# A graph layer on one core: adding stores, list ends on two queues, edges loaded as 112 and 13 rows, keys joined in five passes

## The reference, cut to what matters

```python
xn = _layernorm(x)                                   # x: 6250 nodes x 256
x = x + gnn(xn, edge_index) + mix(xn[None])[0]       # 200000 edges, sorted by dst in the input
x = x + ffn(_layernorm(x)[None])[0]
# gnn: w = sigmoid(relu(xn[col] @ W1 + b1) @ W2 + b2);  sums of w * xn[col] and of w by row, one over the other
# mix: linear attention over 8 heads of 32 columns, one 32x32 product a head over all nodes
# ffn: softmax router, the best two of 6 experts a node, their outputs weighted and summed:
h1 = relu(features @ expert_w1 + expert_b1)          # 256 -> 256, each expert
h2 = relu(h1 @ expert_w2 + expert_b2)
expert_out = h2 @ expert_w3 + expert_b3
combined = sum(expert_out[top_i] * routing_weights)
```

## Time and profile before

| | us |
|---|---|
| median of 3 runs | 1731.37 (1729.7 to 1732.82) |
| the profiled execution | 1728.47 |
| its span, first to last instruction | 1726.7 |
| busy: PE | 1428.3 (83%) |
| busy: DVE | 1354.0 (78%) |
| busy: ACT | 811.1 (47%) |
| busy: POOL | 665.5 (39%) |
| mean granted TensorE clock | 0.925 of full |

### The profile page before, as it was taken

How to read it: one execution, slowest core, us unless ns; L and a number is a source line. 1 busy time by engine, 2 the same in 40 slices (tenths; PEclk the granted TensorE clock), 3 DMA queues, 4 the chain that set the end, 5 groups by cost and what they waited for, 6 DMA issues and landing times.

```text
span 1726.7 us, 40180 instructions
## 1 busy us (share of the span) xinstructions
PE 1428.3 (83%) x12059; PEld 1329.7 (77%) x12059; DVE 1354.0 (78%) x3945; ACT 811.1 (47%) x1983; POOL 665.5 (39%) x669
## 2 busy tenths in 40 slices
PE   0147878646559999999999999999999399999896
PEld 0136777535559999999999999999999399998786
DVE  8998879889958788878888888888887556666565
ACT  1114556336625455555555555555555155555453
POOL 1563565664411222222222222222222323338777
PEclk9767889767779999999999999999999699999998
DMA  7000000003334111111011101110111344433442
GB/s 187 11 1 1 1 1 1 1 18 122 119 105 122 45 41 39 43 41 44 34 49 37 49 34 49 37 48 34 46 40 46 129 135 144 130 102 108 123 129 73
DMA packets 68547, 108.68 MB, mean 63 GB/s; under 512 B 14306, under 2 KB 47849, under 8 KB 68231
## 3 DMA queue, kind: packets, MB, share of 16 engines
q1 hardware_dynamic: 50726, 57.78, 11.9%
q0 software_dynamic: 17760, 50.16, 8.3%
HBM read 52.41 MB, written 57.47 MB: 64 GB/s over the span
## 4 chain that ended last, share of the span: by engine, by line
PE 60%; issue 15%; DVE 11%; POOL 7%; DMA 3%; ACT 1%; SPq 1%; DVEq 1%; another core or an unknown queue 0%; POOLq 0%; ACTq 0%
PE turned L1400 17%; PE front L1400 17%; PE turned L1382 9%; DVE sort_mem L1704 7%; POOL acc_mem L781 6%; PE turned L1541 4%; PE front L1541 4%; PE front L1561 3%; PE front L1429 1%; PE front L1422 1%; PE turned L1534 1%; DMA gath_mem<-in_dst 1%; DVE sort_mem L1801 1%; DVE sort_mem L1712 1%; ACT a_ring L1138 1%
## 5 line engine op out<-in xcount | busy, mean ns | idle before, releaser
L1801 DVE TENSOR_TENSOR sort_mem<-lane_bf,sort_mem 128x512 bf16<-128x512 bf16 x1372 | 519.0, 420 | 145.6 <-PE turned L1382 131.6
L1138 ACT ACTIVATE a_ring<-turned 128x384 fp32r<-128x384 f32 (+1 forms) x686 | 373.4, 544 | 408.9 <-PE turned L1382 405.3
L1400 PE MATMUL turned<-y_all,a_ring 128*128 128x258 f32 x2450 | 387.1, 296 | 8.8 <-ACT a_ring L1138 8.8
L1400 PE MATMUL front<-y_all,a_ring 128*128 128x258 f32 x2352 | 377.4, 297 | 1.1 <-ACT a_ring L1138 1.1
L1704 DVE TENSOR_TENSOR sort_mem<-sort_mem 128x320 f32<-128x320 f32 (+2 forms) x568 | 325.6, 634 | 3.0
L1400 PEld LDWEIGHTS turned<-y_all,a_ring 128*128 128x128 f32 x2450 | 317.5, 190 | 12.9 <-issue 11.2
L1400 PEld LDWEIGHTS front<-y_all,a_ring 128*128 128x128 f32 x2352 | 306.1, 190 | 4.7 <-ACT a_ring L1138 1.4
L1382 PE MATMUL turned<-sort_mem 128*128 128x128 bf16 (+1 forms) x2695 | 259.6, 217 | 3.8 <-DVE sort_mem L1801 2.0
L1382 PEld LDWEIGHTS turned<-sort_mem 128*128 128x128 bf16 x2695 | 139.6, 98 | 40.3 <-DVE sort_mem L1801 9.2
L1339 PE MATMUL turned<-ident,sort_mem 128*128 128x128 f32 x286 | 57.8, 368 | 105.9 <-DVE sort_mem L1704 105.2
L855 POOL TENSOR_TENSOR feat_mem<-feat_mem,ln_eps 128x1 f32<-128x1 f32 x49 | 13.2, 270 | 337.7 <-DVE feat_mem L1865 337.7
(11 more groups left out here) (250 smaller groups left out, 2120.5 us busy)
## 6 DMA issues: line engine op xcount, KB each, us to landing
base<-token_lists SPq DMA_DIRECT2D x54, 258.0 KB
base<-token_lists SPq DMA_DIRECT2D x54, 130.0 KB
gated_rows<-tab_mem SPq DMA_DIRECT2D x49, 128.5 KB, 3.1
late_mem<-mixed_rows SPq DMA_DIRECT2D x49, 128.0 KB
mixed_rows<-base SPq DMA_DIRECT2D x12, 512.0 KB
feat_mem<-in_L_ffn_expert_w SPq DMA_DIRECT2D x18, 256.0 KB, 5.6
base<-in_x SPq DMA_DIRECT2D x1, 3136.0 KB
base<-in_x SPq DMA_DIRECT2D x1, 2352.0 KB
```

The costliest lines, as they stand in the source:

```text
L1138: nc.scalar.activation(a_ring[:, k % 2, :, :].rearrange("p s n -> p (s n)")[:, 0:width], ps_a[k % 2][:, 0:width], ACT.Copy).then_inc(S["a_ ...
L1400: last = nc.tensor.matmul(ps_agg[odd], a_ring[:, k % 2, n, :], y_part(t, part), start=(t == 0 and part == 0), stop=(t == BLOCKS - 1 and pa ...
L1801: nc.vector.tensor_tensor(hot[:, k % 2, 0:pairs, :, :], lane_bf[:, :, :].unsqueeze(1).broadcast_to([P, pairs, P, 2]), edges.unsqueeze(2).b ...
```

## The change

1. The edges are loaded as 112 and 13 rows each instead of 125, with one semaphore for `src` and one for `dst`; `x` part 0 waits for `dst`. The zeros in `base` are written by POOL instead of DVE (`base_zeroed`).
2. The keys are joined in eight passes of DVE instead of nine and two: three for `src_lane`, then five with two inputs each. ACT adds base and sign to `dst` in two passes over half of the columns (`raise_by`), after its three for `dst_lane`; the sign passes over the pad keys run before the edges arrive. An activation of one column stands ahead of ACT's wait for the edges.
3. The last block has its own token row, `list_at` and no wait for `row_listed`; `no_token` and the two spare segments are written during the aggregation; the six ends of the first choice are written three by SP and three by ACT, and POOL writes those of the second choice only after the ninth tile is loaded.
4. Both halves of the experts store to the output, the second with `compute_op` add, so that the DMA adds to the row in DRAM; `first_shares`, `fetch_share` and `first_in` are gone, and DVE's last step in the second half is a product alone.

```diff
-            sp.dma_start(src_in[0:LOAD_ROWS, :], a["src"].rearrange("(p c) -> p c", p=LOAD_ROWS)).then_inc(S["edges_loaded"], 16)
-            sp.dma_start(dst_in[0:LOAD_ROWS, :], a["dst"].rearrange("(p c) -> p c", p=LOAD_ROWS)).then_inc(S["edges_loaded"], 16)
+            for rows in EDGE_PARTS:
+                sp.dma_start(src_in[rows, :], a["src"].rearrange("(p c) -> p c", p=LOAD_ROWS)[rows, :]).then_inc(S["src_loaded"], 16)
+            for rows in EDGE_PARTS:
+                sp.dma_start(dst_in[rows, :], a["dst"].rearrange("(p c) -> p c", p=LOAD_ROWS)[rows, :]).then_inc(S["dst_loaded"], 16)
...
+        def end_lists(engine, regs, first):
+            engine.load(regs[0:EXPERTS // 2], tails[0:1, first:first + EXPERTS // 2].bitcast(I32))
+            for e in range(EXPERTS // 2):
+                at = engine.snap(regs[e], min_val=0, max_val=TOP * SEGMENTS * SEGMENT - P)
+                engine.dma_start(token_lists[bass.ds(at, P), 0:ENDS], no_token[:, 0:ENDS]).then_inc(tails_listed[0], 16)
...
+            act.wait_ge(S["key_step"], 7)
+            dst_pairs, raised = (t.rearrange("p (g t) -> p g t", t=2) for t in (dst_in[0:LOAD_ROWS, :], dst_block))
+            for t in range(2):
+                nc.scalar.activation(raised[:, :, t], dst_pairs[:, :, t], ACT.Identity, bias=raise_by[0:LOAD_ROWS, t:t + 1]).then_inc(S["dst_lane_ready"], 1)
...
-            nc.vector.scalar_tensor_tensor(srcs, src_block, float(2 ** (BLOCK_SHIFT - LANE_BITS)), src_lane, ALU.mult,
-                                           ALU.add).then_inc(S["key_step"], 1)
-            nc.vector.tensor_scalar(srcs, srcs, LANE_BITS, KEY_BASE, ALU.logical_shift_left, ALU.bitwise_or).then_inc(S["key_step"], 1)
-            nc.vector.scalar_tensor_tensor(dst_block, dst_lane, -float(BLOCKS), dsts, ALU.mult, ALU.add).then_inc(S["key_step"], 1)
-            nc.vector.scalar_tensor_tensor(dsts, dst_block, float(2**DST_SHIFT), dst_lane, ALU.mult, ALU.add).then_inc(S["key_step"], 1)
-            nc.vector.tensor_tensor(keys[1][0:LOAD_ROWS, 0:LOAD_COLS].bitcast(I32), srcs, dsts, ALU.bitwise_or).then_inc(S["key_step"], 1)
+            dve.wait_ge(S["dst_lane_ready"], 4)
+            nc.vector.scalar_tensor_tensor(srcs, src_lane, float(P), dst_lane, ALU.mult, ALU.add).then_inc(S["key_step"], 1)
+            dve.wait_ge(S["dst_lane_ready"], 6)
+            nc.vector.scalar_tensor_tensor(dst_block, dst_lane, -float(BLOCKS), dst_block, ALU.mult, ALU.add).then_inc(S["key_step"], 1)
+            nc.vector.scalar_tensor_tensor(dsts, src_block, float(BLOCK_MASK + 1), dst_block, ALU.mult, ALU.add).then_inc(S["key_step"], 1)
+            nc.vector.scalar_tensor_tensor(edge_keys.bitcast(I32), dsts, DST_SHIFT, srcs, ALU.logical_shift_left, ALU.bitwise_or).then_inc(S["key_step"], 1)
...
-            def store_share(m, s, to, last_row):
+            def store_share(m, s, adding):
                 pool.wait_ge(S["out_ready"], m + 1)
...
+                nc.gpsimd.indirect_dma_start(out=out, out_offset=id_of(s), in_=tok[:, s, X2_AT:X2_AT + DIM], in_offset=None,
+                                             bounds_check=NODES - 1, oob_is_err=False,
+                                             compute_op=ALU.add if adding else ALU.bypass).then_inc(tok_stored[s], 16)
...
-            for s in range(AHEAD):
-                fetch_share(firsts, s)
...
-                if k:
-                    dve.wait_ge(first_in[s % PACK_SLOTS], 16 * (FFN_UNROLL // PACK_SLOTS * i + s // PACK_SLOTS - FFN_TILES // PACK_SLOTS) + 16)
...
+                if k == 0:
+                    nc.vector.scalar_tensor_tensor(own, tok[:, row, 0:DIM], share, own, ALU.mult, ALU.add).then_inc(S["out_ready"], 1)
+                else:
+                    nc.vector.tensor_scalar(own, tok[:, row, 0:DIM], share, None, ALU.mult).then_inc(S["out_ready"], 1)
```

More of the change, by code:

```diff
@@ L363, in gps_layer @@
         src_lane, dst_lane, dst_block = (early(LOAD_COLS)[0:LOAD_ROWS, :] for _ in range(3))
-        src_block = keys[0][0:LOAD_ROWS, 0:LOAD_COLS]
+        src_block, edge_keys = (k[0:LOAD_ROWS, 0:LOAD_COLS] for k in (keys[1], keys[0]))
         late = [0]
@@ L374, in gps_layer @@
         packs = after(EXPERTS * PACK).rearrange("p (e n) -> p e n", e=EXPERTS)
-        token_row = [after(TOKEN) for _ in range(2)]
+        token_row = [after(TOKEN), after(TOKEN), late_mem[:, 2 * DIM:2 * DIM + TOKEN]]
         xn2, x2 = ([row[:, at:at + DIM] for row in token_row] for at in (0, X2_AT))
@@ L520, in gps_layer @@
         tok_loaded = [sem(f"tok_loaded{s}") for s in range(FFN_SLOTS)]
-        first_in = [sem(f"first_in{s}") for s in range(PACK_SLOTS)]
         tok_stored = [sem(f"tok_stored{s}") for s in range(FFN_SLOTS)]
@@ L648, in _ @@
             load_mixed(FULL - 2, FULL, 0, FULL)
+            sp.wait_ge(S["no_token_ready"], 3)
+            for k in range(TOP):
+                at = (k * SEGMENTS + EXPERTS) * SEGMENT
+                sp.dma_start(token_lists[at:at + P, :], no_token).then_inc(S["none_listed"], 16)
             sp.wait_ge(S["flag_ready"], 1)
@@ L1606, in _ @@
             nc.vector.tensor_scalar(sign[:, 1:2], row_odd[:, :], 2.0, -1.0, ALU.mult, ALU.add).then_inc(S["key_step"], 1)
+            nc.vector.tensor_scalar(raise_by[:, 0:1], row_odd[:, :], SIGN_RAISE, BASE_RAISE, ALU.mult, ALU.add).then_inc(S["key_step"], 1)
+            nc.vector.tensor_scalar(raise_by[:, 1:2], row_odd[:, :], -SIGN_RAISE, SIGN_RAISE + BASE_RAISE, ALU.mult, ALU.add).then_inc(S["key_step"], 1)
+            dve.wait_ge(S["key_step"], 5)
+            flat, signed = (t.rearrange("p (g t) -> p g t", t=2) for t in (keys[1], keys[0]))
+            for t in range(2):
+                nc.vector.tensor_scalar(signed[:, :, t], flat[:, :, t], sign[:, t:t + 1], None, ALU.mult).then_inc(S["key_step"], 1)
             nc.vector.tensor_scalar(slot[:, :], row_no[:, :], SLOT_ROWS - 1, None, ALU.bitwise_and).then_inc(S["slot_step"], 1)
```

128 lines of the change are left out of this document (59 added, 69 removed).

## The result

| | before | changed |
|---|---|---|
| median of the runs (4 each) | 1732.09 us | 1710.55 us (1702.4 to 1712.45) |
| the profiled execution | 1728.47 | 1709.64 |
| its span | 1726.7 | 1707.9 |

What follows compares the result with a forecast made beforehand. Bounds: edge loads short of engines, PE and DVE in aggregation, list ends delaying the first tile load, POOL in the experts' second half. Gains 8.0 + 5.7 + 18.3 = 32.0 us gave a median of 1699, range 1694 to 1706.

Steps and rivals of the forecast that it cites:

- Edges and keys: Start of the kernel: faster edge loads and fewer key passes start the sort at 21.7 instead of 29.75, 8.0 us gained.
- it is free at about 9.1: Start of the kernel: DVE finishes its setup at about 9.1 us and then begins the passes over the edges.
- It lasts: Front stage: the 8.0 us gained before the sort are kept, since everything behind is relative to DVE.
- rival B: Front: late loads or the front stage's loops give part back; 3 us remain of 8, 1704 us, chance 0.06.
- Aggregation: Stage with PE and DVE in lockstep, between front and experts: the change touches nothing in it, 0 us gained.
- rival I: Aggregation in the fifth experiment: the three parts together slow it where none does alone, 816 us or more.
- The gap: Between aggregation and experts: first tile load at 1372.4 instead of 1378.07, 5.7 us gained, bounds 4 and 6.5.
- The experts: Second half and tail: without fetches PE sets the pace again; 19.8 us gained less 1.5 at the end, net 18.3.
- A: Experts' second half: an adding row costs POOL fetch and store together, 3.1 us a tile stay; median 1717.7, chance 0.12.
- C: Experts' second half: adding stores don't overlap, PE waits for tile loads; 3.86 us a tile, 1751 us, chance 0.08.
- D: Experts' second half: a period between 3.42 and 3.55 us cancels the 32 us; no measurable change, chance 0.02.
- the mixed forms of A: Experts' second half: outcomes between the forecast and A, lying between 1706 and 1718 us.

Runs made afterwards that it cites:

- the filler: Kernel with late zeros plus eight extra PE products of constants at the end of each round of the front; ratio 0.991.
- late zeros: Changed kernel with POOL's memset of `base` held back until DVE has made `src_block`; ratio 0.984, and 0.987 when run again on another chip.
- Each part alone: Three kernels: the kernel before with only the adding stores, only the list ends, or only edges and key passes; ratios 0.992, 0.998, 0.999.
- the fifth experiment: The changed kernel run again, unedited, on another chip; ratio 0.983 to the kernel before.
- edges alone: The kernel before with only the edge loads and key passes (parts 1 and 2); ratio 0.999.

## Why the prediction was right in sign and 10 us off in size

**Edges and keys: loads right, "it is free at about 9.1" nearly right, the next step wrong.** The forecast said first pass at about 9, DVE free at 9.1. The pass was issued at 9.45 and done at 14.79. The failed step is the sentence that the zeros come from POOL "after its constants at 8.5 and for some 6 us": it priced them for SP, which waits for them, and not for DVE, which runs beside them. The term was forecast at 8.0, with bounds 6.2 and 9.0, and measured 3.7. With the memset moved it is 7.2 to 8.0 in five traces, so the rest of the sum stands: 5.3 to 6.1 for the loads, passes of 1.82 with two inputs also for the integer form, and the sort 12.4 behind `dst`, where the sum had 9.2 to 21.7. The prediction also gave an estimate by the Trainium skill's fit, with `dst` 2 us sooner. The page DMA: Bandwidth & Descriptors gives this fit in "Anatomy of one DMA — SWDGE (gpsimd) path", for transfers that GpSimd issues, and here SP issues them. The traces don't bear it out: with the split loads ACT started on `dst` at 9.33 at the earliest.

**"It lasts": at least in large part, and hidden by a spread I hadn't priced.** DVE's statistics of part 1 start at 51.42 instead of 55.09, without a wait, so there the whole gain is still kept. Over the rest the front stage gives back 5.3 us in the two traces, and rival B seemed to have won. Over the thirteen traces without the filler the first `keep_sums` lies at 388.9 + 1.41 x first exchange + 0.417 x time at the lower clock in the front (microseconds, least squares; standard errors 0.15 and 0.053), no trace off by more than 2.4. The slope on the first exchange is not below one, which speaks for what is gained ahead of the sort being kept. That it lies above one is at least partly luck: of the four traces with late zeros and split loads three are of the fastest execution of their kernel (without these three the slope is 1.0, standard error 0.3). Whole times give a lower slope. Over the means of the 14 kernels and chips without the filler (123 executions), fitted with a constant for each chip and for each of parts 3 and 4, it is 0.7 (standard error 0.2): neither nothing nor surely all. The time at the lower level (1.2 GHz) was 204.8 to 232.1 us in these traces, 215.0 in that of before and 225.3 in that of the changed kernel; 10.3 x 0.417 is 4.3 of the 5.3. In the two traces it sits in DVE's gaps, which are 2.0 us more, and in its exchange passes, which are 3.9 us more (398.4 of busy time against 394.5; some passes are stretched by 0.73 or 0.85 us where they meet POOL's operations on two inputs), while its copies are 0.8 less. Over the thirteen traces it is the gaps alone: they reach from 50.7 to 64.6 us and correlate with the stage's length at 0.96, while DVE's busy time stays within 429.8 to 433.7. Within the kernel before the clock shows from run to run: over 23 runs on one chip, span and mean granted clock correlate at -0.65, with spans from 1700.8 to 1714.0. These are correlations. The filler run says that raising the clock is not enough, so clock and front may both follow from how PE's rounds fall against DVE's turns, which is not shown.

**Aggregation, forecast unchanged: 3.5 us longer, open.** Each part alone left it at 812.5 to 812.9 on one chip, and all three with late zeros at 813.2 there, so rival I (of the fifth experiment) is out on that chip. In all other traces it is 833 to 839. Windows from 600 to 1300 us of the kernel before, of the changed one, and of the one with edges alone:

```profile
600.00:1300.00 700.00, 689.48 (x6645) 651.21 (x6644) 570.81 (x2210) 359.82 (x826) 175.70 (x263) 1.00 0.12 42
```

```profile
600.00:1300.00 700.00, 686.82 (x6621) 648.54 (x6620) 568.96 (x2207) 357.46 (x823) 174.95 (x260) 1.00 0.12 42
```

```profile
600.00:1300.00 700.00, 699.30 (x6830) 666.78 (x6829) 584.06 (x2274) 369.66 (x851) 182.36 (x267) 1.00 0.12 43
```

PE stands still for 10.5, 13.2 and 0.7 us. On the slow chips it is about 0.4 us every 34.7 us, once in each round of the loop over two blocks, and in the changed kernel five times some 0.53 more. A round takes 33.8 us on the fast chip, so the pauses are less than half of the difference of 0.9, and the rest lies in work that the rows count as busy. What PE waits for there no view shows, and whether the changed program has more of it by its nature or by the run could not be settled: there is one trace of before on such a chip.

**The gap: 5.1 against 5.7, right.** The wait for the listing goes (0.26 behind another DVE instruction is left of 0.72, and the last block is 0.46 earlier against ACT). Ends and table: the first load is 3.8 us earlier against the tails, where 5.0 were forecast. The mis-sized step is the issue: three issues took 3.19 us on either engine and not 1.8, and each third one stood for about 2 us. Why it stood is open; in the other traces with two issuing engines it is now the second and now the third, for 0.6 to 2.3 us. The load itself is 0.65 shorter. That ACT's part is worth under 1 us was wrong: without it the gap is some 2.2 us longer.

**The experts: 18.9 against 18.3, right.** The pace is PE's, and the run without adding shows that the adding is not in it. Rivals A, C and D fall with the period of 2.897. The terms don't all fit as well as their sum: the second half gave 15.7 of 16.0, the first half lost 0.2, and 0.9 came from where the forecast had nothing, between the first product and the third layer of tile 0 (7.9 us instead of 8.7; 7.3 to 8.8 over all traces). Behind tile 104 the changed kernel gains 2.5, where the forecast had 3.8 less 1.5. Of these 1.5, 0.57 of longer issue and 0.3 of later end behind the last store are seen against the kernel before. The longer landing in the kernel without adding stays unexplained.

**Sum.** Of the 13 us between forecast and the two profiled executions, 4.3 are POOL's memset, 5.3 the front stage, 3.5 the aggregation, 0.6 the gap; the experts gave 0.6 more. Of these only the first is shown to be the change's doing. In the later runs the change gained 29.5 and 20.4 us by the medians, on two chips. Why these differ is open, as there is no trace of the kernel before on either. Rival B's time, 1704, was nearer than the forecast, but not by its mechanism; the mixed forms of A, from 1706 on, include the measured time, and the period rules them out.

**A version beyond both.** Late zeros start the sort 3.5 to 4.4 us earlier than the changed kernel, which the five traces show each time. The whole times are 1681.9 us against 1710.7 for the kernel before on one chip, and 1709.0 against 1711.0 for the changed kernel on another: faster than before, and not proven faster than the changed kernel.

## What to carry to other kernels

Where work is moved to GpSimd, look at what VectorE runs in the same microseconds, not only at who waits for the result: a memset shut out `tensor_scalar` passes for its full length and let those with two inputs by. A stage whose engines meet by chance (an in-order engine that serves two masters) has a spread of its own; price it before reading a difference of 5 us from two traces, by a fit over several. An effect that is small beside it, like 4 us here, is read from the instruction that moved and not from the whole time.

## What was unexpected of the hardware

- Chips differ: the same kernel took 1710.7, 1731.4 and 1738.8 us on three. The aggregation took 812.5 to 813.2 us in four traces on the first and 834.6 to 838.7 in eight on the others. The kernel with late zeros has a trace on two of them: 813.2 and 834.6 us, in spans of 1674.2 and 1692.1.
- A short `tensor_scalar` pass of VectorE took 4.60 us instead of 0.18 beside a memset of GpSimd, and the profile shows no wait.
- An indirect store with adding keeps POOL for 1.55 to 1.57 us undisturbed, one without 0.98; 51 tiles took the same time with either.
- A second engine that issues raised the DMA's rate from 184 to 230 GB/s to as much as 373 in the middle of six transfers of 258 KB.
- Eight extra products a round raised the granted clock from 0.83 to 0.90 over 250 us, and the stage became 15 us longer than in the same kernel without them on the same chip.
